# Epsilon and mean of the norms on VectorE, and a rearranged setup and end, in a fused delta-rule and FFN block

## The reference

```python
x  = layernorm_plain(L0_attn_x)                    # one norm ahead of the attention part
a  = x + delta(layernorm(x, dn_g, dn_b))           # delta rule: keys, triangular solve, scores
b  = a + relu(layernorm(a, mn_g, mn_b) @ w1 + b1) @ w2 + b2
x2 = L0_attn_x + b
h  = silu(n @ w_gate.T / 127) * (n @ w_up.T / 127) # n = layernorm_plain(x2), hidden width 768
out = x2 + h @ w_down.T / 127
```

## Time and profile before

| | |
|---|---|
| median of 3 runs | 1634.22 us (1633.17 to 1639.21) |
| profiled execution | 1637.62 us, span of its instructions 1635.9 us |
| TensorE busy | 1606.2 us, 98% of the span |
| weight loads busy | 1452.8 us, 89% |
| VectorE busy | 1130.1 us, 69% |
| GpSimd busy | 814.5 us, 50% |
| ScalarE busy | 776.9 us, 47% |
| DMA | mean 109 GB/s; 214 to 370 GB/s in the key stage, about 72 in the main loop |

### The profile page before, as it was taken

The page is one execution under the profiler, slowest core; times in us unless marked ns, Lnnn a source line. Parts: engine busy times, 40 slices in busy tenths (PEclk is TensorE's granted clock), DMA queues, the critical chain, the costliest instruction groups (busy, mean ns, idle before and its releaser), DMA issues.

```text
span 1635.9 us, 30028 instructions
## 1 busy us (share of the span) xinstructions
PE 1606.2 (98%) x10758; PEld 1452.8 (89%) x10758; DVE 1130.1 (69%) x2715; ACT 776.9 (47%) x1501; POOL 814.5 (50%) x1176
## 2 busy tenths in 40 slices
PE   8999999899999999999999999999999999999998
PEld 7899998789999899999898989998989899989987
DVE  5777773477777667777776677777776666666664
ACT  5667664344444444444444444444444444444442
POOL 5556872344444554444445544444444444444441
PEclk9999998899999999999999999999999999999999
DMA  6988998212222222222222222222222222222200
GB/s 214 370 277 284 315 306 269 59 59 72 72 72 72 92 89 71 71 71 72 72 72 87 93 67 71 70 68 70 72 94 73 72 72 71 72 72 72 70 14 27
DMA packets 148588, 178.20 MB, mean 109 GB/s; under 512 B 77781, under 2 KB 130264, under 8 KB 140248
## 3 DMA queue, kind: packets, MB, share of 16 engines
q1 hardware_dynamic: 148440, 176.28, 32.7%
HBM read 98.64 MB, written 77.59 MB: 108 GB/s over the span
## 4 chain that ended last, share of the span: by engine, by line
PE 72%; DVE 7%; POOL 2%; ACT 1%; issue 1%; POOLq 0%; DVEq 0%; ACTq 0%
PE ps L174 27%; PE ps L1060 22%; PE ps L1070 9%; PE ps L980 7%; PE ps L974 4%; PE ps L991 3%; DVE work L1364 2%; DVE bs L1378 2%; POOL sc L1547 1%; DVE wt L1348 1%; DVE work L1371 1%; DVE z_lo L1393 1%; DVE mv L1354 0%; PE ps L246 0%; POOL sc L1550 0%
## 5 line engine op out<-in xcount | busy, mean ns | idle before, releaser
L1596 POOL TENSOR_TENSOR hl<-late,hh 128x512 fp32r<-128x512 f32 x128 | 165.3, 1291 | 206.5 <-ACT hh L1223 206.5
L1070 PE MATMUL ps<-wdT,hh 128*128 128x256 f32 x768 | 203.9, 302 | 0.6 <-ACT late L1218 0.6
L1223 ACT ACTIVATE hh<-late 128x512 fp32r<-128x512 f32 x192 | 120.8, 629 | 163.5 <-DVE late L1388 163.5
L1227 ACT ACTIVATE z_hi<-ps 128x256 fp32r<-128x256 f32 x128 | 48.9, 382 | 296.8 <-PE ps L991 296.8
L1070 PE MATMUL ps<-wdT,hl 128*128 128x256 f32 x768 | 187.1, 281 | 2.0 <-DVE hl L1393 2.0
L1388 DVE TENSOR_TENSOR late<-ps,late 128x512 f32<-128x512 f32 x192 | 132.5, 690 | 74.6 <-PE ps L1060 73.1
L1218 ACT ACTIVATE late<-ps 128x512 f32<-128x512 f32 x192 | 113.6, 592 | 126.1 <-PE ps L1060 126.1
L1578 POOL TENSOR_TENSOR xhm_lo<-xh,xhm_hi 128x1024 fp32r<-128x1024 f32 x32 | 76.4, 2388 | 170.0 <-DVE xhm_hi L1460 170.0
L1060 PE MATMUL ps<-xh3T_hi,wgT 128*128 128x512 f32 x384 | 153.7, 400 | 1.1 <-DVE xh3T_lo L1393 1.1
L1060 PE MATMUL ps<-xh3T_lo,wuT 128*128 128x512 f32 x384 | 152.2, 396 | 0.0
L1060 PE MATMUL ps<-xh3T_lo,wgT 128*128 128x512 f32 x384 | 152.1, 396 | 0.0
(11 more groups left out here) (213 smaller groups left out, 4794.7 us busy)
## 6 DMA issues: line engine op xcount, KB each, us to landing
xhT_scratch<-xhTk SPq DMA_DIRECT2D x32, 1024.0 KB, 7.1
xhT<-xhT_scratch SPq DMA_DIRECT2D x32, 1024.0 KB, 6.2
gg_scratch<-late SPq DMA_DIRECT2D x32, 640.0 KB, 4.2
gg<-gg_scratch SPq DMA_DIRECT2D x32, 640.0 KB, 4.0
xk<-in_L_attn_x_dram SPq DMA_DIRECT2D x32, 512.0 KB, 5.7
xt<-in_L_attn_x_dram SPq DMA_DIRECT2D x32, 512.0 KB, 4.0
out_dram<-late SPq DMA_DIRECT2D x32, 512.0 KB, 2.9
low_scratch<-late SPq DMA_DIRECT2D x128, 16.0 KB, 2.9
```

The costliest lines, as they stand in the source:

```text
L1070: mm = pe.matmul(ps[:, (FG, FU)[j // 2], (j % 2) * C:(j % 2 + 1) * C], part[:, h, blk(j)], wdT[:, h, :], start=(h == 0 and part is hh), st ...
L1223: act.activation(hh[:, h, :], hf[:, h % 2, :], ACT.Copy).then_inc(hh_ev[h], 1)
L1596: pool.tensor_tensor(hl[:, h, :], hf[:, h % 2, :], hh[:, h, :].bitcast(F32), ALU.subtract).then_inc(hl_ev[h], 1)
```

## The change

- **Norms of the main loop.** VectorE adds epsilon to the variance itself, right after the aggregation (`dve_eps`), and for norm 2 also negates the mean. `pool_rstd` leaves GpSimd the power; for norm 2 the product with the negated mean stays there. Norm 3 has no product: L1371 now subtracts the mean and multiplies by the power. In norm 2 the two waits on the earlier transposes move behind the product.
- **Order on VectorE.** Step 4 of the inverse moves from before L1371 to behind it. L1371 also waits for the transposes of norm 2 (long past).
- **Last turns.** In turn NS GpSimd's add of `xa` and `a0` waits for the remainders of norm 2's transposes, and ScalarE takes the next gate activation ahead of the copy of the block before. In turn NS + 1 the down product goes over hidden blocks 0 to 4 for all four token blocks first, in four PSUM banks, and then over block 5. The last sequence's output is stored in two halves.
- **Setup.** The key bias comes in as two columns and is added where `kcol` is evacuated, in place of a row with one-row matmuls; `kcol` is made behind the statistics of sequence 1; ScalarE runs one small activation at the very start.
- **Weight preparation.** The shift of q and v is made as four columns (matmuls against `diff`) and added as a bias where the transposed weights are evacuated, in place of 24 matmul records that made it a full matrix and two adds on GpSimd.

The diff, cut to its core:

```diff
@@ -320,8 +323,13 @@
                                       ALU.mult).then_inc(diff_bc_done, 1)
                 for k in range(CB):
                     dve.tensor_scalar(wg[:, k, :], wall[:, k, 0:C], dcol[:, 0, k:k + 1], None, ALU.mult).then_inc(wg_done, 1)
+                dve.tensor_scalar(kbias[:, 1, :], kbias[:, 0, :], 1.0 / C, None, ALU.mult).then_inc(kbias_done, 1)
+
+            def setup_kcol(dve):
+                dve.wait_ge(kbias_done, 1)
                 dve.wait_ge(kcol_ps, 1)
-                dve.tensor_scalar(kcol[:, :], ps[:, P0, 0:CB], 1.0 / C, None, ALU.mult).then_inc(kcol_done, 1)
+                dve.scalar_tensor_tensor(out=kcol[:, :], in0=ps[:, P0, 0:CB], scalar=1.0 / C, in1=kbias[:, 1, :],
+                                         op0=ALU.mult, op1=ALU.add).then_inc(kcol_done, 1)
...
+                act.wait_ge(ones_set, 1)
+                act.activation(spare[:, :], ones[:, 0:TB], ACT.Identity)
...
+                if q == 0:
+                    dve.wait_ge(bqv_done, 1)
+                    dve.wait_ge(w_shift_ps, 1)
+                    dve.scalar_tensor_tensor(out=qcol[:, :], in0=ps[:, T0 + 1, 0:QV // P], scalar=1.0 / C, in1=bqv[:, 1, :],
+                                             op0=ALU.mult, op1=ALU.add).then_inc(w_shift_done, 1)
...
@@ -759,11 +774,6 @@
 
             def prep_pool(pool, q):
 
-                if q == 0:
-                    pool.wait_ge(scaled, CB)
-                    pool.wait_ge(w_shift_done, 1)
-                    for k in range(CB):
-                        pool.tensor_tensor(wfold_qv[:, k, :], wscaled[:, k, :], shift_qv[:, :], ALU.add).then_inc(w_fold_done, 1)
...
@@ -786,9 +795,12 @@
                     act.wait_ge(b1_ps, 1)
                     act.activation(b1w[:, :], piece(0)[:, 0:CB], ACT.Copy).then_inc(b1_sb, 1)
                 if q in (2, 3):
+                    act.wait_ge(w_shift_done, 1)
                     act.wait_ge(tq_ps, q - 1)
-                    act.activation(four((wqT, wvT)[q - 2][:, :, :].rearrange("p a b -> p (a b)")), pieces,
-                                   ACT.Copy).then_inc(tq_done, 1)
+                    for o in range(CB):
+                        op = act.activation((wqT, wvT)[q - 2][:, o, :], ps[:, T0 + 1, o * C:(o + 1) * C], ACT.Identity, scale=1.0,
+                                            bias=qcol[:, CB * (q - 2) + o:CB * (q - 2) + o + 1])
+                    op.then_inc(tq_done, 1)
...
                         for k in range(CB):
-                            pe.matmul(piece(b), diff_bc[:, k, :], wqv[:, k, b * P:(b + 1) * P], start=(k == 0), stop=False)
-                        mm = pe.matmul(piece(b), ones[0:1, :], bqv[:, b * P:(b + 1) * P], start=False, stop=True)
+                            mm = pe.matmul(ps[:, T0 + 1, b:b + 1], wqv[:, k, b * P:(b + 1) * P], diff[:, k:k + 1],
+                                           start=(k == 0), stop=(k == CB - 1))
                     mm.then_inc(w_shift_ps, 1)
...
+                def pe_last(pe, i):
+
+                    for blocks in (range(HB - 1), (HB - 1,)):
+                        for j in range(TB):
+                            for h in blocks:
+                                for part, made in ((hh, hh_ev), (hl, hl_ev)):
+                                    if j == 0:
+                                        pe.wait_ge(made[h], i - 1)
+                                    mm = pe.matmul(ps[:, LAST[j], 0:C], part[:, h, blk(j)], wdT[:, h, :],
+                                                   start=(h == 0 and part is hh), stop=(h == HB - 1 and part is hl))
+                            if j % 2 and h == HB - 1:
+                                mm.then_inc(fo_ps[j // 2], 1)
+
                 def pe_body(pe, i, att, mlp, down, m, r):
+                    if i == NS + 1:
+                        pe_last(pe, i)
+                        return
...
+                    if mlp and not att:
+                        act_silu(act, i, 0)
+                        for h in range(1, HB):
+                            act_silu(act, i, h)
+                            act_hh(act, i, h - 1)
+                        return
...
+                def dve_eps(dve, n_done, mv_, mvd, ls, done):
+                    dve.wait_ge(mvd, n_done)
+                    dve.tensor_scalar(ls[:, 0, :], mv_[:, :, 1], EPS, None, ALU.add).then_inc(done, 1)
...
-                        op = dve.tensor_scalar(xn[:, j, :], x2s[i % 2][:, j, :], sc3[:, 0, j:j + 1], sc3[:, 1, j:j + 1],
-                                               ALU.mult, ALU.add)
+                        op = dve.tensor_scalar(xn[:, j, :], x2s[i % 2][:, j, :], mv3[:, j, 0:1], sc3[:, 0, j:j + 1],
+                                               ALU.subtract, ALU.mult)
...
@@ -1471,16 +1516,20 @@
                     if mlp:
                         dve_x2_stats(dve, i, 1)
                         dve_stats(dve, i, bs3, mv3, bn3, mv3_done)
+                        dve_eps(dve, i, mv3, mv3_done, ls3, l3)
                     if att:
                         dve_z(dve, i, 1)
-                    dve_invert(dve, m, r, 3, 5)
+                    dve_invert(dve, m, r, 3, 4)
                     if mlp:
                         dve.wait_ge(ln3_done, i)
+                        for k in range(CB):
+                            dve.wait_ge(t2_ps[k], i)
                         dve_xh3(dve, i, range(2))
                     if att:
                         dve_w(dve, i, 0)
                     if mlp:
                         dve_xh3(dve, i, range(2, TB)).then_inc(xh3_done, 1)
+                    dve_invert(dve, m, r, 4, 5)
...
                             dve.wait_ge(a0_ev[j], i + 1)
                             dve.bn_stats(bs2[:, j, :], a0[:, j, :]).then_inc(bn2[j], 1)
                         dve_stats(dve, i + 1, bs2, mv2, bn2, mv2_done)
+                        dve_eps(dve, i + 1, mv2, mv2_done, ls2, l2[0])
+                        dve.tensor_scalar(ls2[:, 1, :], mv2[:, :, 0], -1.0, None, ALU.mult).then_inc(l2[1], 1)
...
-                def pool_norm(pool, n_done, read, n_read, mv_, ls, sc, steps, mvd, done):
-
-                    for k in range(CB):
-                        after(pool, read[k], n_read)
-                    pool.wait_ge(mvd, n_done)
-                    pool.tensor_tensor(ls[:, 0, :], mv_[:, :, 1], eps4[:, :], ALU.add).then_inc(steps[0], 1)
-                    pool.tensor_tensor(ls[:, 1, :], zero4[:, :], mv_[:, :, 0], ALU.subtract).then_inc(steps[1], 1)
-                    pool.wait_ge(steps[0], n_done)
-                    pool.tensor_tensor(sc[:, 0, :], ls[:, 0, :], mhalf4[:, :], ALU.pow).then_inc(steps[2], 1)
-                    pool.wait_ge(steps[1], n_done)
-                    pool.wait_ge(steps[2], n_done)
-                    pool.tensor_tensor(sc[:, 1, :], sc[:, 0, :], ls[:, 1, :], ALU.mult).then_inc(done, 1)
+                def pool_rstd(pool, n_done, ls, eps_done, sc, done):
+                    pool.wait_ge(eps_done, n_done)
+                    pool.tensor_tensor(sc[:, 0, :], ls[:, 0, :], mhalf4[:, :], ALU.pow).then_inc(done, 1)
 
                 def pool_body(pool, i, att, mlp, down, m, r):
                     if i == 1:
                         pool.wait_ge(wt_ps, FFN_STEPS)
                     if mlp:
-                        pool_norm(pool, i, t3_ps, i - 1, mv2, ls2, sc2, l2, mv2_done, ln2_done)
+                        pool_rstd(pool, i, ls2, l2[0], sc2, l2[2])
+                        pool.wait_ge(l2[1], i)
+                        pool.wait_ge(l2[2], i)
+                        pool.tensor_tensor(sc2[:, 1, :], sc2[:, 0, :], ls2[:, 1, :], ALU.mult).then_inc(ln2_done, 1)
+                        for k in range(CB):
+                            after(pool, t3_ps[k], i - 1)
                         pool.wait_ge(ln2_done, i)
...
+                        if not att:
+                            for k in range(CB):
+                                pool.wait_ge(t2_ev[k], i)
...
-                        pool_norm(pool, i, t2_ps, i, mv3, ls3, sc3, l3, mv3_done, ln3_done)
+                        pool_rstd(pool, i, ls3, l3, sc3, ln3_done)
...
                         store_out(sp, n)
-                    sp.wait_ge(out_st, 16 * NS)
+                    for half in range(2):
+                        sp.wait_ge(ot_ev[half], NS)
+                        sp.dma_start(out_v[NS - 1][:, 2 * half:2 * half + 2, :], ot[:, 2 * half:2 * half + 2, :]).then_inc(out_st, 16)
+                    sp.wait_ge(out_st, 16 * (NS + 1))
```

More of the change, by code:

```diff
@@ L380, in setup_pe @@
                     pe.matmul(ps[:, P0 + 1, 0:2], diff_bc[:, k, :], wall[:, k, C:KW], start=(k == 0), stop=False)
-                pe.matmul(ps[:, P0 + 1, 0:2], ones[0:1, :], brow[:, C:KW], start=False, stop=True).then_inc(lrow_ps, 1)
+                pe.matmul(ps[:, P0 + 1, 0:2], ones[0:1, :], brow[:, :], start=False, stop=True).then_inc(lrow_ps, 1)
                 pe.wait_ge(wkT_ev, CB)
@@ L1413, in dve_out @@
                         after(dve, out_st, i - 2, 16)
```

(6 more changed lines are left out.)

41 lines of the change are left out of this document (21 added, 20 removed).

## The result

The changed kernel takes 1629.48 us (median of 18 runs, 1628.1 to 1633.11) for 1634.23 before (18 runs): ratio 0.9969, 95% interval 0.9961 to 0.9977, so 4.75 us less where 3.4 was forecast. It stays within the 0.5% that was called the same.

What follows compares the result with a forecast made beforehand. TensorE's issue order was taken as the bound, other engines counting only where it waits. Terms +10.2 -5.9 -1.7 -2.4 +0 -3.5, and -0.1 for turn 1, gave -3.4 from 1634.22: 1630.8 us, range 1623 to 1638.

Steps and rivals of the forecast that it cites:

- Norm 2: Main loop: two operations new on VectorE before the up product make TensorE 0.34 us later in thirty turns, +10.2 us.
- norm 2 is cheap: Rival, 20%: the two VectorE operations slip into hidden gaps, at 0.16 us or below; about 1623 us.
- Norm 3: Main loop: a shorter GpSimd chain brings the z matmul 0.19 us earlier in 31 turns, -5.9 us.
- The slower turns: Nine longer main-loop turns: six lose GpSimd's lateness (1.6 us), three keep a copy's cost (+1.4); together -1.7 us.
- The moved inverse step: Main loop, 18 turns: product L207 moved behind L1371, in front of the z remainder, costs nothing.
- The rival: Shared port, 5%: L207 waits for GpSimd's add, losing 2.2 us in 18 turns, +40, so 1671 us.
- Key stage: Weight preparation: 24 matmul records become 16, -2.5 us; with the bias columns' queue cost, together -2.4 us.
- +0.1: Key stage: the bias read as columns, some 750 elements of 4 bytes more for the queues, costs 0.1 us.
- Turn 1: Second turn of the main loop: a separate small gain of 0.1 us.
- Head: Kernel start: earlier table load, `kcol` at about 10.3 against ScalarE's start at 10.5; 0 us.
- Turn NS, gate, down, output: Last turns: faster `hl` -1.6, gate activation first -0.8, last block's work last -0.7, output in two transfers -0.4; together -3.5 us.
- The clock: TensorE's half-speed stretches around the main loop's start may grow or shrink; 0, with 2 us to each side.

Runs made afterwards that it cites:

- e1: The changed kernel with norm 2's epsilon and negated mean on VectorE behind the up product instead of in front; 1620.71 us, ratio 0.9918.
- e2: The changed kernel with norm 2 wholly back on GpSimd and norm 3 left as changed; 1623.58 us, ratio 0.9939.
- e8: The kernel before with only norm 3's two waits for norm 2's transposes moved from GpSimd to VectorE, in front of L1371; 1631.2 us, ratio 0.9974.
- e3: The changed kernel with norm 3's operations back on GpSimd, the two moved waits staying on VectorE; 1633.23 us, ratio 0.9996.
- e5: The changed kernel with the moved inverse step one place later, behind the last z remainder; 1659.26 us, ratio 1.0140.
- e7: The kernel before with only the last two turns changed, including the output in two transfers; 1631.34 us, ratio 0.9974.
- e0: The changed kernel measured and profiled once more, unchanged; 1631.83 us, ratio 0.9979.
- e6: The changed kernel with the inverse step back in front of norm 3's rows; 1630.19 us, ratio 0.9969.
- e9: e1 with the fold's bias read as a row and added by four small matmuls, and the last down product reordered; 1623.51 us, ratio 0.9931.
- e4: e1 with more filler matmuls, seven at the end of the key stage and nine in turn 1; 1623.92 us, ratio 0.9927.
- e11: e1 with the last down product reordered so the output's first half completes earlier; 1622.01 us, ratio 0.9929.

## Why the prediction was right, and where it wasn't

The forecast of 3.4 us less lies between the two measurements of the same kernel, 4.75 and 2.3. Part by part it was right in most places and wrong in some, and in part the errors cancelled.

*Norm 2* (+10.2 forecast) costs 0.27 us a turn, 8.1 in 30 turns (e1 and e2 against the changed kernel). The mechanism and its place were right; the term was too large because the up product starts 0.28 later, not 0.34: the second operation follows the first at 0.077 and the product the second at 0.103, where I had allowed 0.16. The rival "norm 2 is cheap" would have needed 0.16.

*Norm 3* (-5.9): L1412 at 1.34 after the aggregation, `wt` held by TensorE's matmul, z segment 0.19 shorter: all as forecast. But I put the whole of it down to the operations that left GpSimd. e8 and e3 show that 0.09 of the 0.19 are the two waits that the diff moves to VectorE. They stand in the diff, and I mentioned them only as a possible cost ("L1371 now has two more waits"). What a wait costs on the engine that it leaves was missing from the working.

*The slower turns* (-1.7): 3.3 us of them became 1.3. Six are gone, as forecast, but not thanks to slack behind `wt`: GpSimd's late starts are gone already in e8, where only the two waits are moved and the rest of the chain is unchanged. Whether the waits caused them is not shown. The three with the copy still stand, 0.43 to 0.47 for 0.46 to 0.47; +1.4 was forecast for them against 1.5, right.

*The moved inverse step* (0): L207 starts 0.25 before the add in all 18 turns and takes 0.2 to 0.4. The rival's condition was read rightly. Of its price, 2.2 a turn, the 0.4 that TensorE was to absorb was wrong: in e5, where the step starts later and so waits less, a delay of 1.3 makes the turn 1.33 longer.

*Key stage* (-2.4): 9.37 for 11.81 between transposes 9 and 10, in every profile of this preparation at full clock. But from the first key transpose to turn 0 the seven profiles with this preparation, the full clock and no added fillers have a mean of 259.4 us, the four with the old one 260.6: only 1.2 less. The other half is lost elsewhere in the stage. "+0.1" for the bias read as single elements is one term that stays open, between none and about 1 us; no row stood behind it.

*Turn 1* (-0.1): 0.9 and 1.8 us shorter in the two profiles. I had called what GpSimd saves in norm 2 worthless, and here TensorE waits for its rows, which come 0.4 earlier. That is not all of it: e2, with these rows as late as before, took 44.31 too, and the clock is at half for a part of the turn. The rest stays open.

*Head* (0): `kcol` is made at 10.32, forecast 10.3; the head is 0.06 shorter.

*Turn NS, gate, down, output* (-1.6, -0.8, -0.7, -0.4): 6.01 to 4.41 makes -1.60 (e7); 12.31 to 11.53 makes -0.78; from the first down matmul to the end of the last output sum 7.58 became 6.91, -0.67; from there to the end 3.40 became 2.74, -0.66. Missing was norm 2's own gain in turn NS, -0.2 net: it is worthless in the turns in which L980 stands in front of the transposes, and not in this one.

*The clock* (0, 2 to each side) was the largest single difference between the two profiles, 3.6 us in turn 0. It fell there in three of the 14 profiles (before, e0, e6: 33.7 to 33.9 us), in e9 for a part of the turn (31.5), and not in ten others of both kinds (30.2). In turn 1 it fell in all 14; in e3, e5 and e9 the granted clock over that turn is 0.86 for 0.92 or 0.93, and it took 47.2 to 48.0 us for at most 46.0. What decides it is open: e4 left a gap of TensorE in turn 1.

So norm 2 cost 2.1 less than forecast, the slower turns, the last turns and turn 1 gave 0.3, 0.4 and about 1 more, and the key stage gave 1.2 less. By the profiles that would be some 2.5 us below the forecast. The two medians lie 1.35 below it and 1.1 above it: two measurements of one kernel differ by as much as these errors, and the clock in turn 0 alone moves an execution by 3.6 us. That the total came out so near was therefore partly luck.

## What to carry to other kernels

When small operations move to an engine, look for that engine's next idle time, not for the earliest legal place: two operations of 0.16 us in front of a product on the path cost 8 us in 30 turns, and behind it nothing. When a diff moves waits, price them on both engines: extra waits in front of a short chain on GpSimd cost 0.09 us each time, and moving two of them was worth 4.2 us in 29 turns, late turns included. When an experiment is to fill a gap, look in its trace whether another gap is left. Before a difference of two profiles is explained, cut both at the same instructions and set aside the stretches whose granted clock differs; and measure the changed kernel twice before the last microsecond is explained.

## What was new about the hardware

- GpSimd starts a first operation 0.079 us after the semaphore's giver with one wait, 0.170 with a separate wait instruction in front (e8 has both).
- Single instructions start 0.29 us (GpSimd) or 0.35 us (VectorE) later than in the other turns, in the same turns in every profile of the same order. The cause is open.
- VectorE's operation behind an add of GpSimd waits for all of it, one-input copy included (2.56 for 1.07 us); started first, the copy keeps its 1.07 and the add takes 3.08 for 2.40.
- TensorE's clock can fall to half with no gap on TensorE in the profile: in e9 among 24 records of one column, in e11 behind 16 of them, and in eight other profiles with these 16 not.
- Fillers at the end of a stage in which TensorE ends last delay the next stage by their own length (1.6 us), and the gap between the stages stays (1.75 us).
